# Four-layer graph network on one core: source terms of layer 1's edge scores moved to VectorE, layer 3's first message and its LayerNorm transposes moved up, plan costs booked ahead

## The reference, cut to what matters

```python
# x: 64 batches of 256 nodes x 128 features; adj: 256 x 256, shared by all batches and all layers
def layer0(x, adj):                       # x is relu(layernorm(x))
    pre = s1[:, :, None, :] + s2[:, None, :, :] + b_lin     # s1, s2 from adj's rows times x; e = 256
    h = where(pre >= 0, pre, 0.2 * pre)                     # for every pair of nodes (i, j)
    e = einsum('bije,e->bij', h, a) + adj
    return sigmoid(softmax(e, 2) @ x)
def layer1(x, adj):
    x_h = elu(x @ Wi + bi)
    a_src = x_h @ We[:H, 0]                # the source terms
    a_tgt = x_h @ We[H:, 0]                # the target terms
    e = sigmoid(a_tgt[:, :, None] + a_src[:, None, :] + be[0]) * mask(adj)
    agg, self_part = e @ x_h, x_h * sum(e, -1)
    return concat(elu(concat(agg, self_part) @ Wn + bn), x_h) @ Wm + bm
def layer2(x, adj): ...                    # attention masked by adj, tanh-limited logits
def layer3(h, adj):                        # 5 steps of a gated unit
    for _ in range(5):
        m = adj @ h; z, r = sigmoid(...), sigmoid(...); hv = tanh(...); h = (1 - z) * h + z * hv
    return h
for layer in (layer0, layer1, layer2, layer3):
    x = x + layer(relu(layernorm(x)))
```

## Time and profile before

| | |
|---|---|
| median of 3 runs | 5592.85 us (5590.37 to 5593.27) |
| the profiled execution's own time | 5579.68 us |
| its span | 5577.9 us, mean granted TensorE clock 0.988 |
| TensorE matmul busy | 5428.9 us, 97% |
| VectorE, ScalarE, GpSimd busy | 5093.6, 5086.3, 4831.1 us (91%, 91%, 87%) |
| HBM | 3 GB/s over the span |

### The profile page before, as it was taken

One profiled execution on the slowest core, in us unless ns is written; L12 is line 12 of the kernel. 1 busy time (PEld: TensorE's weight loads), 2 busy tenths in 40 slices (PEclk: granted clock), 3 DMA queues, 4 the chain that ended last, 5 costly groups with the idle time before them and its releaser, 6 DMA issues.

```text
span 5577.9 us, 115796 instructions
## 1 busy us (share of the span) xinstructions
PE 5428.9 (97%) x38790; PEld 2133.7 (38%) x38790; DVE 5093.6 (91%) x9843; ACT 5086.3 (91%) x13332; POOL 4831.1 (87%) x9606
## 2 busy tenths in 40 slices
PE   8999999999999999999999999999999999999997
PEld 2333333333333333333333433333333333333334
DVE  8999999999998999999999999999999999999993
ACT  8999999999999999999999999999999999999993
POOL 8988888889888888889888888888898888889880
PEclk9999999999999999999999999999999999999998
DMA  0000000000000000000000000000000000000000
GB/s 14 3 4 7 7 6 3 6 7 7 6 7 3 6 7 7 6 3 6 7 7 6 5 4 7 7 7 6 3 6 7 7 6 3 6 7 7 6 6 6
DMA packets 44233, 33.97 MB, mean 6 GB/s; under 512 B 4736, under 2 KB 39552, under 8 KB 43648
## 3 DMA queue, kind: packets, MB, share of 16 engines
q1 hardware_dynamic: 43648, 26.56, 1.6%
HBM read 9.77 MB, written 8.39 MB: 3 GB/s over the span
## 4 chain that ended last, share of the span: by engine, by line
PE 93%; POOL 2%; DVE 2%; issue 2%; ACT 1%; DMA 0%; SPq 0%; POOLq 0%; DVEq 0%
PE S L1108 58%; PE R L1052 15%; PE S L1052 5%; PE W L1052 4%; PE V L1052 3%; PE R L1250 3%; POOL ring L570 2%; PE R L1258 1%; PE S L1099 1%; ACT ring L902 1%; PE V L1135 1%; DVE ring L699 1%; POOL signed L561 1%; PE R L1147 1%; PE W L1147 0%
## 5 line engine op out<-in xcount | busy, mean ns | idle before, releaser
L902 ACT ACTIVATE ring<-V,U_minus 128x256 f32<-128x256 f32 x10496 | 4114.8, 645 | 5.6 <-issue 5.6
L1108 PE MATMUL S<-ring,a_window 128*32 128x512 f32 x30720 | 3493.8, 598 | 107.9 <-issue 79.6
L570 POOL TENSOR_SCALAR ring<-W,U 128x256 f32<-128x256 f32 x7040 | 3424.6, 501 | 19.6 <-PE S L1108 19.6
L699 DVE TENSOR_TENSOR ring<-U,W 128x1024 f32<-128x1024 f32 (+2 forms) x2592 | 2662.7, 1064 | 7.1 <-ACT V L926 7.1
L1108 PEld LDWEIGHTS S<-ring,a_window 128*32 128x32 f32 x30720 | 914.4, 110 | 2396.8 <-issue 2349.2
L561 POOL TENSOR_SCALAR signed<-W_signed,U_ceiling,U_floor 128x256 f32<-128x256 f32 x2048 | 1166.5, 571 | 105.2 <-DVE ring L690 104.9
L694 DVE TENSOR_TENSOR ring<-U,W 128x256 f32<-128x256 f32 x2176 | 854.5, 409 | 0.1
L690 DVE SCALAR_TENSOR_TENSOR ring<-W,U,signed 128x256 f32<-128x256 f32 x2048 | 825.0, 470 | 2.2 <-POOL signed L561 2.2
L532 POOL TENSOR_TENSOR rstd<-var,minus_half 128x4 f32<-128x4 f32 (+1 forms) x160 | 148.8, 930 | 309.6 <-DVE var L725 171.6
L1052 PE MATMUL R<-mT,W 128*128 128x512 f32 (+1 forms) x640 | 334.0, 604 | 2.7 <-ACT mT L1012 2.7
L1052 PE MATMUL R<-AT,h 128*128 128x256 f32 x1264 | 326.9, 404 | 2.1 <-ACT h L1024 2.1
(11 more groups left out here) (185 smaller groups left out, 4282.7 us busy)
## 6 DMA issues: line engine op xcount, KB each, us to landing
X<-in_x SPq DMA_DIRECT2D x64, 128.0 KB, 2.1
X_held<-X SPq DMA_DIRECT2D x32, 256.0 KB, 2.4
out<-OUT SPq DMA_DIRECT2D x64, 128.0 KB, 1.9
edge<-in_L_gnn_w_w SPq DMA_DIRECT2D x3, 128.0 KB, 2.1
A<-in_adj SPq DMA_DIRECT2D x1, 256.0 KB, 2.7
Wn<-in_L_gnn_Wn SPq DMA_DIRECT2D x1, 128.0 KB, 2.5
Wm<-in_L_gnn_Wm SPq DMA_DIRECT2D x1, 128.0 KB, 2.5
weight<-in_L_gnn_u_w SPq DMA_DIRECT2D x2, 64.0 KB, 2.1
```

The source lines that it names most:

```text
L570: last = gp.tensor_scalar(ring[:, place, g, half * N:(half + 1) * N], W[:, y, c], LARGEST, U[:, y, c, i:i + 1], ALU.min, ALU.max)
L699: piece = dve.tensor_tensor(ring[:, place, g:g + groups].rearrange("p g (h j) -> p g h j", h=NB), u.unsqueeze(3).to_broadcast([P, groups, ...
L902: last = act.activation(ring[:, place, g, half * N:(half + 1) * N], W_scalar[y][:, c * N:(c + 1) * N], ACT.Relu, bias=U_minus[:, y, c, i:i ...
L1108: last = pe.matmul(S[y][g * ROWS:(g + 1) * ROWS, :], a_window[:, c, ROWS - 1 - row:2 * ROWS - 1 - row], ring[:, place, g], start=False, st ...
```

## The change: what it does

1. The four one-column matmuls go. The column's first half is loaded once, broadcast over the partitions (`We_src`), and VectorE at a new stage, source (lot 43), makes each of the four `src_bias` columns in one pass of product and sum over `xh` and `We_src`. It waits for ScalarE's copy `xh` where it waited for TensorE. The target `exp1` of the product is scratch. The stages behind move: tanh from lot 42 to 44, mask from 45 to 46, halves from 46 to 47; aggregate stays at 49.
2. LN3's transposes and the first message of layer 3 move from stage 118 to 115, the copy of h3T from 120 to 118; the last step's output on VectorE moves from lot 113 to 112.
3. `stage_costs` books half of each cost three lots ahead, and several costs are other numbers (ScalarE's norm 15.4 for 10, a source stage of 8, GpSimd's start per lot 0.1 for 1.0). Over a turn the blocks go from 412 to 402 for VectorE, from 328 to 321 for ScalarE and from 220 to 237 for GpSimd.

```diff
-L1 = dict(..., edge_terms=40, edge_copy=42, tanh=42, mask=45, halves=46, aggregate=49, ...)
+L1 = dict(..., edge_terms=40, edge_copy=42, source=43, tanh=44, mask=46, halves=47, aggregate=49, ...)
-LN3 = dict(stats=107, factors=109, norm=111, transpose=118, copy=120)
-L3_FROM, L3_PERIOD = 118, 25
-L3 = dict(message=0, ..., transpose=21, back=23)
+LN3 = dict(stats=107, factors=109, norm=111, transpose=115, copy=118)
+L3_FROM, L3_PERIOD, L3_FIRST_MESSAGE = 118, 25, 115
+L3 = dict(message=0, ..., transpose=21, out=22, back=23)
...
-LOADS0, LOADS_REST = 3, 21
+LOADS0, LOADS_REST = 3, 22
...
-VECTOR_BLOCK, ..., POOL_BLOCK, POOL_START, VECTOR_SUMMED, POOL_SIGNED = 2.67, 0.69, 3.57, 4.5, 1.0, 3.92, 5.33
+VECTOR_BLOCK, ..., POOL_BLOCK, POOL_START, VECTOR_SUMMED, POOL_SIGNED = 2.67, 0.69, 3.57, 4.5, 0.1, 3.92, 5.3
+AHEAD = 3
...
         for name, cost in stages.items():
-            costs[at + table[name]] += cost
+            book(costs, at + table[name], cost)
+
+    def book(costs, t, cost):
+
+        costs[t % LOTS] += cost / 2
+        costs[(t - AHEAD) % LOTS] += cost / 2
...
-        put(scalar, POST[h], half, exp=10, copy=4.8, tanh=5)
+        put(scalar, POST[h], half, exp=8, copy=3, tanh=5)
...
+        book(pool, half, 7)
     for ln in (LN1, LN2, LN3):
         put(vector, ln, 0, stats=12.5)
-        put(scalar, ln, 0, norm=10, copy=4.8)
+        put(scalar, ln, 0, norm=15.4, copy=4.8)
...
-    put(vector, L1, 0, elu=10, edge_copy=1.3, mask=12, agg_copy=6, recv_elu=10, residual=6)
+    put(vector, L1, 0, elu=10, source=8, mask=12, agg_copy=6, recv_elu=10, residual=6)
...
         def layer3_at(turn, t):
-            pair = turn.m - 1 if t >= L3_FROM else turn.m - 2
-            step, p = divmod((t - L3_FROM) % LOTS, L3_PERIOD)
+            pair = turn.m - 1 if t >= L3_FIRST_MESSAGE else turn.m - 2
+            if t == L3_FIRST_MESSAGE:
+                step, p = 0, L3["message"]
+            else:
+                step, p = divmod((t - L3_FROM) % LOTS, L3_PERIOD)
+                if step == 0 and p == L3["message"]:
+                    step = STEPS
...
+            load(We_src[:], L1_We.rearrange("k o -> (k o)")[0:P].partition_broadcast(P))
...
+                    dve.tensor_scalar(be[:], be[:], 0.5, None, ALU.mult)
...
-                if t == L1["edge_copy"]:
-                    dve.wait_ge(edge_psum, pair)
-                    dve.tensor_scalar(src_bias[:], side[1][:, SRC_COLS], be[:], 0.5, ALU.add, ALU.mult).then_inc(src_ready, 1)
+                if t == L1["source"]:
+                    dve.wait_ge(xh_ready, pair)
+                    for n in range(4):
+                        last = dve.tensor_tensor_reduce(exp1[:, n * P:(n + 1) * P], xh[:, n], We_src[:], 0.5, be[:],
+                                                        ALU.mult, ALU.add, accum_out=src_bias[:, n:n + 1])
+                    last.then_inc(src_ready, 1)
...
-                    if p == L3["back"] and s == STEPS - 1:
+                    if p == L3["out"] and s == STEPS - 1:
...
-            def pre(p, y, value, bank_read=None, src_read=None):
+            def pre(p, y, value, bank_read=None):
                 if p == PRE[1 - y]["transpose"]:
-                    if src_read is not None:
-                        pe.wait_ge(*src_read)
                     pe.wait_ge(h0_ready, value)
...
                     mm(S[1][:], We_tgt_wide[:], xhT[:])
-                    for n in range(4):
-                        mm(side[1][:, SRC_COLS.start + n:SRC_COLS.start + n + 1], xhT[:, n * P:(n + 1) * P], We[:, 0:1])
                     for n in range(4):
                         last = pe.transpose(W_bank[1][:, n * P:(n + 1) * P], xhT[:, n * P:(n + 1) * P], ident[:])
```

More of the change, by code:

```diff
@@ L97 @@
 LN1 = dict(stats=20, factors=22, norm=23, transpose=28, copy=29)
-L1 = dict(shift=24, project=32, exp=34, elu=35, edge_terms=40, edge_copy=42, tanh=42, mask=45, halves=46, aggregate=49, agg_copy=52, receive=56, recv_exp=58, recv_elu=59, out=61, residual=63)
+L1 = dict(shift=24, project=32, exp=34, elu=35, edge_terms=40, edge_copy=42, source=43, tanh=44, mask=46, halves=47, aggregate=49, agg_copy=52, receive=56, recv_exp=58, recv_elu=59, out=61, residual=63)
 LN2 = dict(stats=64, factors=66, norm=68, transpose=70, copy=72)
 L2 = dict(project=78, copy=81, scores=86, tanh=89, exp=90, mask=93, aggregate=103, residual=106)
-LN3 = dict(stats=107, factors=109, norm=111, transpose=118, copy=120)
-L3_FROM, L3_PERIOD = 118, 25
-L3 = dict(message=0, copy=3, gates=5, reset=9, update=11, candidate=13, z_gate=15, tanh=16, state=19, transpose=21, back=23)
+LN3 = dict(stats=107, factors=109, norm=111, transpose=115, copy=118)
+L3_FROM, L3_PERIOD, L3_FIRST_MESSAGE = 118, 25, 115
+L3 = dict(message=0, copy=3, gates=5, reset=9, update=11, candidate=13, z_gate=15, tanh=16, state=19, transpose=21, out=22, back=23)
 def layer3_lot(s, stage):
     return (L3_FROM + s * L3_PERIOD + L3[stage]) % LOTS
-SRC_COLS = slice(2 * N - 4, 2 * N)
-LOADS0, LOADS_REST = 3, 21
+LOADS0, LOADS_REST = 3, 22
 SETUP_REST = dict(vector_raw=12, transpose=14, vector_turned=20, product=24, vector_product=30, ready=34)
@@ L147, in stage_costs @@
     for s in range(STEPS):
-        for stage, cost in dict(update=6, state=18).items():
-            vector[layer3_lot(s, stage)] += cost
+        for stage, cost in dict(update=7, state=18, out=6 if s == STEPS - 1 else 0).items():
+            book(vector, layer3_lot(s, stage), cost)
         for stage, cost in dict(copy=4.8, reset=5.7, z_gate=5.7, tanh=5.7, back=4.8 if s < STEPS - 1 else 0).items():
-            scalar[layer3_lot(s, stage)] += cost
+            book(scalar, layer3_lot(s, stage), cost)
     return vector, scalar, pool
```

8 lines of the change are left out of this document (4 added, 4 removed).

## The result

The changed kernel takes 5500.94 us (median of 6 runs, 5497.01 to 5503.92), the kernel before in the same comparison 5593.83 us (5590.37 to 5596.93): ratio 0.9833, 95% interval 0.9821 to 0.9846. The forecast was 5474 us, 0.979 of the runs shown before: 27 us too low, inside its range. The profiled execution took 5497.01 us, its span 5494.9.

The account below looks back on a forecast made before the run. TensorE's own program was taken as the bound, with pauses. Like turns 4.4 us shorter (128 us), 10 us lost early: 119 us off 5579.7 gives 5461, plus 13 for the median, 5474 us; range 5442 to 5550 us.

Parts of the forecast that it names:

- The pause at lot 115: TensorE's idle between lots 114 and 115, behind ScalarE's evacuation: 2.7 us a turn goes, with 0.3 us to spare.
- the clock and the short wait: TensorE's lower clock after the pause and a short wait before lot 114: 1.4 us a turn goes, 0.2 kept for the clock.
- ScalarE late in lots 115 to 120: Fourteen blocks plus the copy of h3T make TensorE wait 0.3 us a turn, between 0 and 1.2.
- One-column matmuls: Eight one-column records on TensorE's path go: 0.8 us a turn less.
- Source passes: Four VectorE passes at lot 43, 0.27 us each, 1.1 us together, bounded by 0.9 and 1.7 us; no cost taken.
- the spare 1.4 us of lot 50: GpSimd's nine blocks of lots 48 to 50 end 1.4 us before TensorE starts lot 50.
- TensorE waits for GpSimd at lots 48 to 50: Listed sign of being wrong: the later edge mask sets GpSimd's blocks back; the forecast took no cost there.
- slower rival: The late edge chain stalls TensorE at lots 48 to 50 every turn, clock falling there: 5663 us, chance 0.05.
- VectorE is not fuller than before: Source passes add 1.1 us to VectorE, the ten blocks it hands over take off 2.3 us.
- rival at 168.5 us a turn: GpSimd, with 157.3 us of work and about 11 of waits, bounds the like turns: 5530 us, chance 0.11.
- Early turns: GpSimd has little room in turns 0 and 1: 7 us more (0 to 8) and 3 more (-1 to 6).
- The sum: A like turn falls from 171.0 to 166.6 us, 29 x 4.4 = 128 us less; turns 0 and 1 add 10.

Follow-up runs that it names:

- message alone: The kernel before with only layer 3's stages moved (LN3's transposes and first message, copy, output), source terms and split as before: ratio 0.9846.
- e6: The changed kernel with the copy of layer 3's first message at lot 120 in place of 121: 5524.21 us, ratio 0.9888.
- e5: The changed kernel with two blocks, at lots 106 and 108, handed from GpSimd to ScalarE: 5545.52 us, ratio 0.9939.
- e9: e7 with four blocks of lots 117 and 118 moved from ScalarE to VectorE, two back at each of lots 121 and 122: 5455.64 us, ratio 0.9775.
- e7: The changed kernel with the edge mask at lot 45 and the halves at 46, one lot sooner each: ratio 0.9820.
- The plan alone: The kernel before with only the changed kernel's split of the blocks (402, 237, 321): ratio 0.9898.

## Why the prediction was right, and where it was off

- **The pause at lot 115** (-2.7 us, and -1.4 for the clock and the short wait): right. 0.14 us of the pause is left in the mean, records at a lower clock fall from 32 to 9, and the turns' mean lies 0.2 us above the shortest instead of 1.4. The 0.3 us of cover was real but thin: with the old split 0.9 us of pause stays (message alone, 0.9846), so the three blocks fewer on ScalarE, 1.07 us in the working, are needed as it says.
- **ScalarE late in lots 115 to 120** (+0.3, bound 1.2): the mis-sized term. The place and the engine were right; it measured 1.41 us at lots 117 to 120, outside the bound. Two steps failed, about half of the missing 1.1 us each. First, ScalarE's times: I had its norm over at 2004.9 in the times of before, "both sides moved 0.8 us ahead", with GpSimd 0.2 us later at most. In the like turns the norm ended 2.53 us before lot 112's start in the mean and now ends 1.77 before it: 0.76 us later against TensorE and not 0.2. GpSimd comes to the factors 3.7 us after the variances in the mean and no longer 2.7, so ScalarE didn't move ahead with TensorE. Second, the working stops at lot 120's last block and has no term for the copy of the message, `mT`, which the gates behind lot 120 need and which stands behind three more blocks: 0.57 us. e6, the copy sooner, takes these 0.57 us away and leaves the other 0.84; e5, two blocks fewer on GpSimd ahead of the factors, brings ScalarE's norm to 2.60 us before lot 112 and the 1.41 us to about 0.8; and e9, four blocks fewer on ScalarE, lowers the like turn by 0.86 us.
- **One-column matmuls** (-0.8): right, -0.84 at lot 37, as the trace of before had it. That is four times what the issue floor on the Trainium skill's page "TensorE: Matmul & The Clock Gate", section "Back-to-back issue gap", would give. The same section says that in a stream of weight loads and matmuls both set the spacing, so the floor of a matmul by itself was the wrong rule for these eight, each of which has a weight load of 128 columns in the trace of before. But with the passes that replace them they are worth 0.23% alone and not 0.84 x 32 = 27 us, 0.5%: what is won is given back where another engine is late.
- **Source passes** (0.27 us each, bound 0.42): wrong. They start 0.49 us apart beside GpSimd's blocks (median of one 555 ns, least 346), 1.95 us for four and not 1.1. The mask and sum came 5.1 us later against TensorE and not 4.1 (3.3 by the clock of before, 0.8 for TensorE's own move), and the nine blocks behind took 4.54 us and not 4.1: so the spare 1.4 us of lot 50 was used up, and 0.26 us of waiting came. That was the thinnest cover of the working, and it did give way: "TensorE waits for GpSimd at lots 48 to 50" stood among the signs of being wrong, and it holds, at 1/20 of the slower rival's size. e7 shows it, since the earlier mask takes the wait away. The collision also fell on the other engine: the working had four of GpSimd's blocks stretched, but its nine blocks beside the passes took 0.47 us each, and it is VectorE's passes that are longer. "VectorE is not fuller than before" failed too (160.5 us in turn 4 for 157.9).
- **GpSimd** (rival at 168.5 us a turn): the mean turn of 168.04 comes near it, but GpSimd isn't the sole bound: e9 gains 1.3 us a turn on the changed kernel with the same 237 blocks on GpSimd. It is late at two places, at LN3's factors, where it works through ScalarE, and at lot 50. Its work was undersized: 162.7 us in turn 4 where 157.3 was worked out from 17 blocks of 0.454 us.
- **Early turns**: +7 and +3 forecast, +6.0 and +0.7 measured. The plan alone has the same +6.0.
- **The sum**: 3.0 us a turn of 4.4 forecast. 1.1 us of the rest is ScalarE's term, 0.3 lot 50; 29 x 1.44 = 42 us. Against this stand 3.3 us less lost in the early turns and 2.5 more won in the last ones: 36 us, the distance from my 5461 to the profiled 5497. The median lies 4 us above that execution where I took 13, which leaves the 27 us. So the number is nearer than the working: 42 us of error in the like turns was made up for in part by 15 us elsewhere, and that part is luck.
